# Graph network and spiking feed-forward on one core: count blocks without zero products, head one-hots in two sets, one-hots for a step ahead of the copy, spikes counted later

## What is computed

```
msg = h[edge_src]; agg = segment_sum(msg, edge_dst)          # 1250 nodes, 40000 edges, edges sorted by target
layer(h) = h @ W_self + (agg / max(deg, 1)) @ W_neigh + b     # 1024 features
g   = layer1(relu(layer0(layernorm(x))));   x = x + g
y   = square(relu(layernorm(x) @ W_fc.T)) @ W_proj.T          # 4096 hidden
mem = 0.9 * mem + y - (mem > 1); spike = (mem > 1)            # 5 steps
out = x + sum(spikes) / 5
```

## Time and profile before

| | |
|---|---|
| time, median of 3 runs | 1626.48 us (1625.7 to 1627.73) |
| the profiled execution's own time | 1628.24 us |
| its span | 1626.5 us |
| TensorE busy | 1602.5 us of the span |
| VectorE, ScalarE, GpSimd busy | 893.3, 453.6, 103.7 us |
| mean granted TensorE clock | 0.997 |

### The profile page before, as it was taken

One profiled execution on the slowest core, in us unless ns is written; L12 is line 12 of the kernel. 1 busy time (PEld: TensorE's weight loads), 2 busy tenths in 40 slices (PEclk: granted clock), 3 DMA queues, 4 the chain that ended last, 5 costly groups with the idle time before them and its releaser, 6 DMA issues.

```text
span 1626.5 us, 22412 instructions
## 1 busy us (share of the span) xinstructions
PE 1602.5 (99%) x7738; PEld 1346.6 (83%) x7738; DVE 893.3 (55%) x1618; ACT 453.6 (28%) x795; POOL 103.7 (6%) x200
## 2 busy tenths in 40 slices
PE   7999999999999999999999999999999999999998
PEld 5777667788888888889899898998998888888885
DVE  7786777556211322556344343343443688888778
ACT  3344555211111100114032131231321333333256
POOL 0230134300000000001000000000001000000001
PEclk9999999999999999999999999999999999999999
DMA  7322333466523554567222021120213233333223
GB/s 296 134 105 81 102 127 127 173 242 260 201 98 106 207 198 146 191 204 261 115 78 78 26 103 36 67 79 33 95 52 129 104 116 116 116 116 109 101 75 49
DMA packets 55703, 205.45 MB, mean 126 GB/s; under 512 B 5360, under 2 KB 14078, under 8 KB 50084
## 3 DMA queue, kind: packets, MB, share of 16 engines
q1 hardware_dynamic: 52772, 190.19, 33.2%
q0 software_dynamic: 2848, 14.16, 2.7%
HBM read 153.85 MB, written 52.04 MB: 127 GB/s over the span
## 4 chain that ended last, share of the span: by engine, by line
PE 95%; DVE 2%; DMA 1%; issue 1%; ACT 1%; DVEq 0%; POOL 0%; SPq 0%; ACTq 0%; POOLq 0%
PE bank L1654 26%; PE bank L1510 26%; PE bank L1673 24%; PE bank L1603 11%; PE bank L1459 3%; PE bank L1711 2%; PE bank L1486 2%; DVE w L1153 0%; DMA w_landing<-w_self 0%; DMA pr_raw<-w_proj 0%; DMA at_dram<-counts_tile 0%; DMA rows<-x 0%; PE bank L1730 0%; DVE key_hot L1100 0%; DVE stats L1108 0%
## 5 line engine op out<-in xcount | busy, mean ns | idle before, releaser
L1510 PE MATMUL bank<-w,xt 128*128 128x512 f32 x1920 | 462.8, 396 | 2.6 <-DVE w L1153 2.6
L1654 PE MATMUL bank<-x2t,fc_w 128*128 128x384 f32 (+1 forms) x2304 | 438.4, 350 | 0.5 <-ACT relu L925 0.5
L1654 PEld LDWEIGHTS bank<-x2t,fc_w 128*128 128x128 f32 x2304 | 411.7, 188 | 25.7 <-issue 0.8
L1510 PEld LDWEIGHTS bank<-w,xt 128*128 128x128 f32 x1920 | 356.6, 189 | 77.0 <-issue 3.3
L1673 PE MATMUL bank<-pr_w,hid 128*128 128x512 f32 (+1 forms) x1728 | 394.8, 389 | 0.0
L1673 PEld LDWEIGHTS bank<-pr_w,hid 128*128 128x128 f32 (+1 forms) x1728 | 320.6, 186 | 70.8
L1365 DVE TENSOR_TENSOR y<-y,bank 128x512 f32<-128x512 f32 (+1 forms) x144 | 98.8, 687 | 206.9 <-PE bank L1673 206.9
L1603 PE MATMUL bank<-z,at 128*128 128x512 f32 x800 | 186.9, 392 | 0.0
L1603 PEld LDWEIGHTS bank<-z,at 128*128 128x128 f32 x800 | 148.8, 188 | 30.2
L920 ACT ACTIVATE pr_w<-pr_raw 128x1024 fp32r<-128x1024 f32 x64 | 67.1, 1049 | 365.7 <-PE bank L1673 362.6
L1308 DVE TENSOR_TENSOR square<-relu 128x384 f32<-128x384 f32 (+1 forms) x96 | 56.9, 592 | 144.2 <-ACT relu L925 144.2
(11 more groups left out here) (139 smaller groups left out, 972.5 us busy)
## 6 DMA issues: line engine op xcount, KB each, us to landing
fc_raw<-w_fc SPq DMA_DIRECT2D x64, 512.0 KB, 4.3
pr_raw<-w_proj SPq DMA_DIRECT2D x64, 512.0 KB, 3.5
xt<-xt_dram SPq DMA_DIRECT2D x24, 1024.0 KB, 5.0
xt_dram<-xt SPq DMA_DIRECT2D x18, 1024.0 KB, 4.3
at<-at_dram SPq DMA_DIRECT2D x20, 640.0 KB, 5.5
part_dram<-rows SPq DMA_DIRECT2D x20, 512.0 KB, 3.9
rows<-part_dram SPq DMA_DIRECT2D x20, 512.0 KB, 4.3
rows<-x SPq DMA_DIRECT2D x18, 512.0 KB, 5.0
```

Of the source, the lines that this page charges most:

```text
L1510: ins = nc.tensor.matmul(bank[:, 2 * (u % 2) + q, :], xt[j][:, a, k, :], w[:, k, b, q * HALF:(q + 1) * HALF], start=(k == 0 and m == 0), s ...
L1654: ins = nc.tensor.matmul(bank[:, 4 + (c if g == 0 else j % 2), 0:n], fc_w[:, j % 2, k, a, :], x2t[g][:, k, v, c0:c0 + n], start=(k == 0 an ...
```

## The change

Six things change.

1. There are two head sets, `HEAD_SETS = (0, 3)`, used by even and odd blocks in turn, so GpSimd and VectorE can make the next block's head while TensorE still has this one's.
2. The product with `zero_w` is gone. The last product of a block closes the sum: in a block without extra turns the head's third product is kept back and comes behind the loop, in one with extra turns it is the last product of the last turn. ScalarE's copy waits for a set's use instead of for the closing product.
3. In the 17 windows of `SHORT_TURNS`, step 0 takes one chunk from each set instead of two. In a window with extra turns, step 0 now runs the loop's rest and the later steps one full turn each.
4. ScalarE writes a step's one-hots ahead of the copy of the block before it.
5. S0's first unit has two steps from slot 40 instead of three from slot 30; unit 4 of S0 has six steps and units 6 and 7 have seven, where unit 4 had seven and units 6 and 7 six.
6. The spikes of the first six halves are summed behind pieces 6, 7 and 8, two halves each, instead of behind 3, 4, 5, 6, 7 and 8; there are 41 slots for spikes instead of 25, and `rates` come in pairs. The narrow identity is made after G1 by GpSimd.

```diff
-HEAD_SET, LOOP_SETS = 0, (1, 2)
+HEAD_SETS, LOOP_SETS = (0, 3), (1, 2)
+SETS = 4
+HOT_AT = {0: 0, 3: HEAD_CHUNKS, 1: 2 * HEAD_CHUNKS, 2: 2 * HEAD_CHUNKS + LOOP_SET}
...
+SHORT_TURNS = {0, 6, 9, 10, 11, 12, 13, 18, 27, 31} | set(range(33, 40))
...
+def chunks_of_set(i, j):
+
+    return 1 if j == 0 and window_of(i) in SHORT_TURNS else LOOP_SET
...
-        [(A0 + 3, 1, 30, 12)] + [(A0 + n, 3, 14, 36) for n in range(4, TILES - 1)] + [(A0 + 9, 1, 12, 12), (S0, 3, 30, 18)]
-        + [(S0 + p, 6 if p in (6, 7) else 7, 0, 48) for p in range(1, 9)]):
+        [(A0 + 3, 1, 30, 12)] + [(A0 + n, 3, 14, 36) for n in range(4, TILES - 1)] + [(A0 + 9, 1, 12, 12), (S0, 2, 40, 10)]
+        + [(S0 + p, 6 if p == 4 else 7, 0, 48) for p in range(1, 9)]):
...
-        for half in range(RATE_HALVES - 1):
-            COUNT_STAGES[half + 3] += [(half, s) for s in range(STEPS)]
-        COUNT_STAGES[-1] += [(RATE_HALVES - 1, s) for s in range(STEPS)]
+        for half in range(RATE_HALVES):
+            COUNT_STAGES[min(6 + half // 2, len(PIECES) - 1)] += [(half, s) for s in range(STEPS)]
...
-            if j > 0:
-                engine.reg_add(first, first, LOOP_CHUNKS)
-            if j < extra_turns(i):
-                engine.reg_add(stop, first, 1)
-                end = stop
-            latest = CHUNKS + HEAD_CHUNKS - 1 + LOOP_CHUNKS * j
+            latest = CHUNKS + HEAD_CHUNKS - 1
+            if j == 0:
+                latest += LOOP_CHUNKS * extra_turns(i)
+                engine.reg_add(edge, first, LOOP_CHUNKS * extra_turns(i))
+                first = edge
+            else:
+                latest += LOOP_CHUNKS * (j - 1)
+                if j > 1:
+                    engine.reg_add(first, first, LOOP_CHUNKS)
+                engine.reg_add(edge, first, 1)
+                end = edge
...
-            def head_of_block(i, first, end):
-                pool.wait_ge(hot_used[HEAD_SET], i + 1)
+            def head_of_block(pair, side, first, end):
+                pool.wait_ge(hot_used[HEAD_SETS[side]], pair + 1)
...
-                act.wait_ge(counts_summed, i + 1)
+                if extra_turns(i) > 0:
+                    act.wait_ge(hot_used[ACT_SET], closed)
+                else:
+                    act.wait_ge(hot_used[HEAD_SETS[i % 2]], i // 2 + 2)
...
-            for p in range(TILES):
-                for step in steps_of(S0 + p):
-                    src_one_hots(*step)
-                    copy_counts(*step)
+            own_steps = [step for p in range(TILES) for step in steps_of(S0 + p)]
+            src_one_hots(*own_steps[0])
+            for step, before in zip(own_steps[1:], own_steps):
+                src_one_hots(*step)
+                copy_counts(*before)
+            copy_counts(*own_steps[-1])
...
-                for entry in stage:
+                for place, entry in enumerate(stage):
                     if entry != DVE_SPIKE:
                         spike_sign(*entry)
-                if 0 <= p - 3 < RATE_HALVES:
-                    rates(p - 3)
+                    if p == 8 and place in (2, 3):
+                        rates(place + 2)
+                for half in RATES_AT.get(p, ()):
+                    rates(half)
...
             def step_of_edges(i, j):
-                first, end = turns_of_step(pe, registers, stop, i, j)
+                last, head = extra_turns(i), HEAD_SETS[i % 2]
                 if j == 0:
                     if i >= 2:
                         pe.wait_ge(counts_copied, i - 1)
-                    products_of_set(i, HEAD_SET, i + 1, start=True)
-                with pe.Fori(first, end, LOOP_CHUNKS) as g:
-                    for s in LOOP_SETS:
-                        products_of_set(i, s, visit)
-                    pe.reg_add(visit, visit, 1)
-                    pe.reg_add(next_visit, next_visit, 1)
-                if j == extra_turns(i):
-                    nc.tensor.matmul(bank[:, 4 + i % 2, 0:2], zero_w[:, :], iota[0:P, 0:2], start=False,
-                                     stop=True).then_inc(counts_summed, 1)
+                    pe.wait_ge(src_hot_ready, i + 1)
+                    pe.wait_ge(key_hot_ready[head], i // 2 + 1)
+                    kept = 0 if last else 1
+                    for c in range(HEAD_CHUNKS - kept):
+                        ins = product_of_chunk(i, head, c, start=(c == 0))
+                    if not kept:
+                        ins.then_inc(hot_used[head], 1)
+                count = chunks_of_set(i, j)
+                first, end = turns_of_step(pe, registers, edge, i, j)
+                with pe.Fori(first, end, count * len(LOOP_SETS)):
+                    turn_of_edges(i, count, stop=(j == last > 0))
+                if last == 0:
+                    product_of_chunk(i, head, HEAD_CHUNKS - 1, stop=True).then_inc(hot_used[head], 1)
```

More of the change, by code:

```diff
@@ L268, in gnn_ffn @@
         act_hot_ready = sem("act_hot_ready")
-        key_hot_ready = [sem(f"key_hot_ready{s}") for s in range(3)]
-        hot_used = [sem(f"hot_used{s}") for s in range(3)]
-        counts_summed = sem("counts_summed")
+        key_hot_ready = [sem(f"key_hot_ready{s}") for s in range(SETS)]
+        hot_used = [sem(f"hot_used{s}") for s in range(SETS)]
         counts_copied = sem("counts_copied")
@@ L391, in spike_of @@
                 return last_spike[:, :]
-            return spikes[:, SPIKE_ORDER.index((p, s)) % SPIKE_SLOTS, 0:width]
+            slot = SPIKE_ORDER.index((p, s)) % SPIKE_SLOTS
+            return (spikes[:, slot, 0:width] if slot < SPIKE_SLOTS - MORE_SLOTS else
+                    more_spikes[:, slot - SPIKE_SLOTS + MORE_SLOTS, 0:width])
         def raw_w(k):
@@ L716, in _ @@
                 for i in range(2):
-                    head_of_block(2 * pair + i - FIRST_WINDOW, *ranges[i])
+                    head_of_block(pair - FIRST_WINDOW // 2, i, *ranges[i])
             with pool.Fori(0, FIRST_WINDOW // 2) as pair:
@@ L797, in _ @@
             registers = range_registers(act, "act")
-            stop = act.alloc_register("act_stop")
+            edge = act.alloc_register("act_edge")
+            closed = act.alloc_register("act_closed")
             def src_one_hots(i, j):
-                first, end = turns_of_step(act, registers, stop, i, j)
-                with act.Fori(first, end, LOOP_CHUNKS) as g:
+                count = chunks_of_set(i, j)
+                first, end = turns_of_step(act, registers, edge, i, j)
+                with act.Fori(first, end, count * len(LOOP_SETS)) as g:
                     act.wait_ge(act_hot_ready, visit)
-                    for c in range(LOOP_SET):
-                        chunk = g + (LOOP_SET * LOOP_SETS.index(ACT_SET) + c)
+                    for c in range(count):
+                        chunk = g + (count * LOOP_SETS.index(ACT_SET) + c)
                         ins = nc.scalar.activation(dist[:, c, :], iota[0:P, 0:128], ACT.Square,
@@ L847, in _ @@
                     high_of_row(0, n + 1, ACT.Copy)
-                for step in steps[0:1]:
-                    copy_counts(*step)
-                for step in steps[1:]:
+                for step, before in zip(steps[1:], steps):
                     src_one_hots(*step)
-                    copy_counts(*step)
+                    copy_counts(*before)
                 if n + 2 < TILES:
@@ L863, in _ @@
                         src_one_hots(*step)
+                for step in steps[-1:]:
+                    copy_counts(*step)
             for k in range(4):
@@ L1441, in _ @@
         def _(pe):
-            for s in range(3):
+            for s in range(SETS):
                 pe.sem_inc(hot_used[s], 1)
@@ L1449, in _, with product_of_chunk, turn_of_edges @@
             registers = range_registers(pe, "pe")
[L1450 to L1461 removed]
+            edge = pe.alloc_register("pe_edge")
+            def product_of_chunk(i, s, c, start=False, stop=False):
+                return nc.tensor.matmul(bank[:, 4 + i % 2, 0:WINDOW_COLS], src_hot[:, HOT_AT[s] + c, :], key_hot[:, HOT_AT[s] + c, :],
+                                        start=start, stop=stop)
+            def turn_of_edges(i, count, stop=False):
+                for s in LOOP_SETS:
+                    if s == ACT_SET:
+                        pe.wait_ge(act_hot_ready, next_visit)
+                    pe.wait_ge(key_hot_ready[s], visit)
+                    for c in range(count):
+                        ins = product_of_chunk(i, s, c, stop=(stop and s == ACT_SET and c == count - 1))
+                    ins.then_inc(hot_used[s], 1)
+                pe.reg_add(visit, visit, 1)
+                pe.reg_add(next_visit, next_visit, 1)
             def step_of_edges(i, j):
[L1464 removed]
+                last, head = extra_turns(i), HEAD_SETS[i % 2]
                 if j == 0:
```

112 lines of the change are left out of this document (46 added, 66 removed).

## The result

The changed kernel takes 1617.08 us (median of four executions, 1615.95 to 1617.26), beside 1626.15 us for the kernel before (1625.7 to 1627.73). The ratio is 0.9941, 95% interval 0.9929 to 0.9954: 9.1 us faster, where I had forecast 15.95 us with a range up to 1616.5 us. The direction was right, the size was not.

What follows compares the result with a forecast made beforehand. TensorE, busy 1602.5 of 1626.5 us, was taken to bound the kernel. Gains of 4.65 + 4.4 + 3.6 + 1.0 + 2.3 = 15.95 us gave 1610.6 us, with a range of 1606.5 to 1616.5.

Steps and rivals of the forecast that it cites:

- The products left out: Loop turns of the 17 short windows, in A0 and S0: 34 fewer one-hot products at 0.137 us, 4.65 us faster.
- The closing products: End of each of the 40 blocks: the zero product goes, 0.11 us each, 4.4 us faster.
- The start of S0: S0's first count steps, moved to slots 40 and 45: TensorE's wait and the clock's drop go, 3.6 us, bounds 0 and 3.9.
- Wait 1.97, first step 0.99 against 0.72, slow products 1.33 + 0.31: 3.9 us lost: S0's start before the change: TensorE's wait plus products slowed at a granted clock of 0.87, read from one trace.
- The last blocks of S0: Blocks of seven products late in S0: fewer waits for GpSimd and ScalarE, 1.0 us faster, bounds 2.4 and -1.5.
- 0.4 us more: S0's unit 7, with seven steps instead of six: pays a wait behind a taken pair too, 0.4 us more.
- VectorE takes over in S0: Rival: waits behind the taken pair in every unit, or S0's start stall shifts; 1614.1 us; 0.17 jointly with the tail.
- The tail: Spiking tail: pieces every 5.45 us instead of 6.54, VectorE becomes the bound, 2.3 us faster, bounds 1.0 and 3.3.
- all three extra copies: Lower bound in the spiking tail: 2.7 us minus three more copies of rates on ScalarE (0.58 us each), 1.0 us.
- ScalarE bounds the tail: Rival: paired copies of rates eat the tail's gain, leaving 0 to 1.0; 1611.9 to 1612.9 us; 0.17 jointly with VectorE.
- The fetch inside the block: Rival: fetch, index step and branch open gaps in each block, costing 31.4 us, 1642 us; 3 in 100 for slower.

Runs made afterwards that it cites:

- full_turns: The changed kernel with no short windows (SHORT_TURNS empty), so the 34 products come back: 1621.34 us.
- zero_close: The changed kernel with a closing zero product again in the 25 windows without extra turns: 1620.07 us.
- head_waits: The changed kernel with GpSimd beginning a block's head only after TensorE has used that of the block before: 1631.39 us.
- two_tiles: The changed kernel with a second tile of counts, used for the copies and stores of tiles 4, 6 and 8: 1614.59 us, ratio 0.9927.
- early_rates: The changed kernel with ScalarE's six copies of rates moved earlier in the tail's stages 6 to 8: median 1615.60 us.

## Why the prediction was wrong

**The products left out**, 4.65 us forecast, measured 4.2 (full_turns). Right.

**The closing products**, 4.4 us forecast: 0.104 us each between the first two traces, 0.095 in zero_close, 3.8 to 4.2 us. Right. What I hadn't seen is that without the second head set the gain would have turned into a loss: head_waits is 14.3 us slower than the changed kernel and 5.1 slower than the kernel before.

**The start of S0**, 3.6 us forecast, measured 1.51 less 0.55 for the four products that only moved: 1.0 us. The wait shrank, to 0.23 us at the first step, and the clock didn't fall, as said. The step that failed is "Wait 1.97, first step 0.99 against 0.72, slow products 1.33 + 0.31: 3.9 us lost". That is the loss of one traced execution. It was 1.8 us above the median, I saw this, and took the median as equal to the span without asking where the 1.8 us lay. They lay in this very term (1.86 us). A further 0.7 went to weights that land later (6.30 against 5.57 us).

**The last blocks of S0**, 1.0 us forecast, measured 3.20 - 12 x 0.137 - 28 x 0.104 = -1.4 us, at the lower bound that I had given. The mechanisms named were right: unit 8 no longer waits for GpSimd and gave 2.4 us, two_tiles adds 2.3 us and so comes to +0.9, and the wait behind a taken pair stays at 0.8 to 1.0 us in each of the units 5 to 8. What failed is that I moved the steps but not the stores that they carry. I counted unit 7's extra step as "0.4 us more" and left SP's queue out, where three stores went from ahead of a unit's transfers to right behind them. Unit 7 came out 2.1 us longer; with the second tile of counts it is the 0.4. The rival *VectorE takes over in S0* gave 1.0 us for both terms, where they measured 1.0 - 1.4 = -0.4. It came closer than my 4.6, but not by its reason: the new waits are for ScalarE and a transfer.

**The tail**, 2.3 us forecast, measured 3.0 at the last result and 0.1 at the end. The mis-sized term is not VectorE's. I followed the chain to the last result and held the 3.4 us behind it constant. My bound of "all three extra copies" on ScalarE asked what the late copies cost ScalarE, and not what the stores that wait for them cost the end. *ScalarE bounds the tail* gave the size by luck, and not the cause.

**The sum.** 2.6 + 2.4 + 2.2 us too much in these three terms, and 0.3 too little elsewhere: 6.9 of 15.95 us. 5.2 us of it are the change's own doing and not a misread trace: 2.3 for the stores of counts, which two_tiles gets back, and 2.9 at the end, of which early_rates gets back 2.1 in its trace. The fetch inside the block, which I had feared most, costs nothing that a trace shows: a block of seven products takes 0.97 us as before.

## What to carry to other kernels

When a table moves work, move its transfers along in your sum too. The three stores that moved from ahead of a unit's transfers to right behind them took 7.2 us in the median instead of 3.0 here, with the same bytes. Follow a kernel's end to the landing of its output and not to its last result: work that is put off to the end brings its stores with it, and they queue. Before a stall is priced from one trace, look how that execution stands to the median of the timed ones, and in which term the difference lies.

## What was not expected of the hardware

Behind equal waits of 1.68 and 1.70 us at one place of one kernel the granted clock fell to 0.87 over 13 us in one execution and stayed at 1.00 in another. A fall of that kind is worth 1.6 to 1.9 us here (16.82 and 17.10 us against 15.24) and isn't sure to come. Six adding stores of 256 KB on GpSimd's queue, issued in pairs 0.5 to 0.9 us apart, landed 1.4 to 2.5 us apart, so that each 256 KB beyond the first cost about 2.0 us.
